# Computing the first four blocks of a scan's input projections one stage earlier, and passing them through DRAM

## The chip, the cores and the metric

The program runs on one core of a Trainium2 chip. The metric is device time in microseconds (us), the median of three runs. The engines are named PE (TensorE, matmuls), PEld (its weight loads), DVE (VectorE), ACT (ScalarE), POOL (GpSimd) and SP (SyncE, which issues most transfers). Each engine works through its own instructions in order; semaphores join them.

## The reference, cut to what matters

Input x has 4 x 1024 tokens of 256 channels. Eight layers follow each other; each adds to x. The change touches the fourth (a mixture of experts) and the fifth (a selective scan); the sixth runs interleaved with the fifth.

```
x = x + ln(mixture(ln(x)))
x = x + ln(scan_layer(ln(x)))
x = x + ln(ternary_mlp(ln(x)))

def mixture(x):            # 16 experts, the 2 best per token, and one shared
    w, i = top_k(sigmoid(x @ gate_w + gate_b), 2);  w = w / sum(w)
    return x + mlp_shared(x) + sum(w * mlp_i(x))        # mlp: (silu(x@wg) * (x@wu)) @ wd

def scan_layer(x):         # 256 -> 512 channels, 16 states
    xc, z = split(x @ in_proj_w.T)
    xs = silu(conv4(xc) + conv_b)
    dt, B, C = split(xs @ x_proj_w.T)
    dt = softplus(dt @ dt_proj_w.T + dt_proj_b)
    h[t] = exp(dt * A) * h[t-1] + dt * B * xs           # per channel and state
    y = (sum(h * C) + D * xs) * silu(z)
    return y @ out_proj_w.T
```

## The kernel before, in words

x stays in on-chip memory as `chip.x`, 32 tiles of 128 tokens; a block is four tiles (512 tokens), and there are NB = 8 blocks. All data of the parts shown is 32-bit floating point.

**The mixture** (`mixture`) routes the tokens, runs the experts over 80 blocks of gathered rows, and stores their outputs in DRAM as `y_rows`. Then comes its results stage, the one that the change rebuilds. For each block n:

- POOL issues eight indirect gathers (`results(n)`, L2108) that bring the rows of both choices into `got`, which is laid over the experts' up weights (in the trace it bears their name, `l1f_w`).
- PE computes the shared expert (`up`, L1833; `down`, L1841 and L1842). ACT takes the gate (`gate_rows`, L1905) and DVE multiplies (`hidden_rows`, L2034). `down` adds the normalised row (`acc`) by a matmul with the identity.
- DVE's `combine(n)` adds two scaled gathers (L2044) and takes the statistics of the post norm (L1586 to L1591). POOL raises to the power -1/2 (L1595), DVE makes the shift (L1601), ACT applies the norm (L1608) and DVE's `add` adds the result to `chip.x` (L2055).
- POOL's order is: results(0), results(1), then for each n the power of post norm n and results(n+2). At n = 7 it also does the scan's first norm (`following`).

**The scan and its MLP** (`scan_and_mlp`) begin when all engines have left the mixture. A head computes block 0's input: SP loads `w_in` and other weights, ACT normalises block 0 (`pre`, L1570), PE turns it (L3042), projects x (L3054) and z (L3061), ACT makes the 16 diagonals of the conv weights (L3314), DVE convolves (L3431), PE projects to `x_dbl` (L3098) and dt (L3105). `x_dbl`'s B and C rows go through DRAM and come back broadcast (`bc`).

The main loop has iterations n = 0 to 9, of UNITS = 64 units k each. Iteration n runs the scan of block n (states by channel tiles): ACT's exponentials (L3276), POOL's products `dbx` (L2968) and sums (L2978), DVE's scans (L3489) and multiplications by C (L3500). Fixed slots k (the tables `FUSED`, `ZERO`, `FIRST`) put the other work between the units: for block n+1 the pre norm, turning, x projection, convolution, `xs` and dt; for block n the z projection (`project_z`, L3081; ACT takes it with Silu at k = 12) and the gating of y (L3423); for block n-1 the output projection (L3114), post norm and residual, and then the MLP's turning (`turn_l`, L3042), pairs (L3137) and hidden layers (L3150); for block n-2 the rest of the MLP (L3126). Four shared PSUM banks pass PE's results to ACT and DVE. MLP weights stream from DRAM through a ring of four buffers. PE's queue for iteration n is: outputs(n-1), hidden 14 and 15 of n-2, z(n), dt(n), the MLP's output n-2, turn_l(n-1), pairs, and the hidden layers 0 to 12 of n-1 with turn, x projection, `x_dbl` and dt of n+1 among them.

Of the kernel before, what the change touches and what calls it, by code (L numbers as in the profile page):

```python
# [12 lines left out]
F32 = mybir.dt.float32  # L13
# [22 lines left out]
FAR_ROWS = 3 * SEQ_TILES  # L36

# [1596 lines left out]
def mixture(chip, name, gate_w, gate_b, w_up, wd, counts, ids, x_rows, y_rows, norms, following):  # L1634
# [12 lines left out]
    AHEAD = 4  # L1647
    with ExitStack() as ctx:
# [12 lines left out]
        later = [ScaledNorm(chip, s, f"pre{n}") for n in range(2, NB)]  # L1661
        turned_score = s.sb("turned_score", [P, 2, P])
# [27 lines left out]
        normed = wo[:, 1:1 + 2 * BT, :].rearrange("p (i k) d -> p i k d", i=2)  # L1690
        PS = chip.psum
# [19 lines left out]
        summed = s.sem("summed")  # L1711
        normed_ready, added = s.sem("normed_ready"), s.sem("added")
# [3 lines left out]
        def _(sp):  # L1716
# [14 lines left out]
            for b in range(BLOCKS):  # L1731
                sp.wait_ge(b_out, b + 1)
                sp.dma_start(y_rows[b * P:(b + 1) * P, :], out_b[:, b % AHEAD, :]).then_inc(b_put[b % AHEAD], 16)

        @block.tensor
        def _(pe):
# [100 lines left out]
            def down(n):  # L1837
                pe.wait_ge(h_ready, n + 1)
                wait(pe, out_used, n - 1)
                for k in range(BT):  # L1840
                    nc.tensor.matmul(outs[n % 2][:, k, :], chip.ident[:], acc[:, n * BT + k, :], start=True, stop=False)  # L1841
                    last = nc.tensor.matmul(outs[n % 2][:, k, :], h[:, n % 2, k * P:(k + 1) * P], wo[:, 0, :],  # L1842
                                            start=False, stop=True)
                last.then_inc(out_ready, 1)

# [3 lines left out]
            for n in range(NB):  # L1849
                down(n)  # L1850
                if n + 2 < NB:
                    up(n + 2)

        @block.scalar
        def _(act):
# [51 lines left out]
            gate_rows(0)  # L1907
            gate_rows(1)
            for n in range(NB):
                if n + 2 < NB:  # L1910
                    gate_rows(n + 2)
                wait(act, added, n - 1)
                posts[n % 2].scalar(act, n // 2, lambda k: acc[:, n * BT + k, :], lambda k: normed[:, n % 2, k, :])\
                    .then_inc(normed_ready, 1)

        @block.vector
        def _(v):
# [118 lines left out]

            def combine(n):
                v.wait_ge(got_ready[n % 4], 16 * CHOICES * BT * (n // 4 + 1))
                v.wait_ge(out_ready, n + 1)
                for c, (done, rows_of) in enumerate(((out_used, lambda k: outs[n % 2][:, k, :]),  # L2040
                                                     (summed, lambda k: acc[:, n * BT + k, :]))):
                    for k in range(BT):
                        t = n * BT + k
                        last = nc.vector.scalar_tensor_tensor(  # L2044
                            out=acc[:, t, :], in0=got[:, n % 4, c, k, :], scalar=share[:, t, c:c + 1], in1=rows_of(k),
                            op0=ALU.mult, op1=ALU.add)
                    last.then_inc(done, 1)
                    v.drain()
# [3 lines left out]
            def add(n):  # L2052
                v.wait_ge(normed_ready, n + 1)
                x = chip.x[:, n * BT:(n + 1) * BT, :]
                nc.vector.tensor_tensor(x, x, normed[:, n % 2], ALU.add).then_inc(added, 1)  # L2055

            hidden_rows(0)
            hidden_rows(1)
            for n in range(NB):
                if n == NB - 1:  # L2060
                    wait(v, added, 1)
                    following.statistics(v, lambda k: chip.x[:, k, :])
                combine(n)
                if n:
                    posts[(n - 1) % 2].vector(v, (n - 1) // 2)
                if n + 2 < NB:
                    hidden_rows(n + 2)
                if n >= 2:
                    add(n - 2)
            posts[(NB - 1) % 2].vector(v, (NB - 1) // 2)  # L2070
            add(NB - 2)
# [3 lines left out]
        def _(g):  # L2075
# [40 lines left out]
            for n in range(NB):  # L2116
                if n == NB - 1:
                    following.gpsimd(g, 0)
                posts[n % 2].gpsimd(g, n // 2)
                if n + 2 < NB:  # L2120
# [264 lines left out]
def windowed_core(chip, name, stacks, y, window, ahead):  # L2385
# [16 lines left out]
    with ExitStack() as ctx:  # L2402
# [226 lines left out]
    "z": 12,  # L2629
    "soften": [53, 13],  # L2630
# [43 lines left out]
        "turn": 9, "in": [13, 14, 27, 28], "conv": [19, 23, 32, 36], "xp_pe": 41, "dt_pe": 47}  # L2674
# [4 lines left out]
def scan_and_mlp(chip, name, a, m, pre, bias, following):  # L2679
# [22 lines left out]
    with ExitStack() as ctx:  # L2702
# [26 lines left out]
        first_loaded, xc_cleared = s.sem("first_loaded"), s.sem("xc_cleared")  # L2729
# [1041 lines left out]
```

## Time and profile before

| | |
|---|---|
| median of 3 runs | 4317.69 us (4316.76 to 4327.96) |
| the profiled execution's own time | 4321.57 us |
| its span | 4319.8 us |
| mean granted clock of TensorE | 0.963 |
| PE busy | 3980.5 us, 92% of the span |
| DVE busy | 3322.9 us, 77% |
| ACT busy | 2849.1 us, 66% |
| POOL busy | 2003.2 us, 46% |

Stages by time from the span's start: the mixture's experts end near 1423 us, its results stage runs to 1530.8 us, the scan's head from there to the first scan at 1570.9 us, the scan and MLP loop to about 3125 us. Busy shares are averages over stages with different limits, so each stage is to be read by itself. A row of a timeline gives start, duration, engine, line, operation, output and inputs, and in brackets how long the engine sat idle before it and what it waited for.

### The profile page before, as it was taken

How to read it: one execution, taken by the hardware profiler on the slowest of the kernel's cores; microseconds unless marked ns; L12 is line 12 of the kernel's file. 1: busy time of each engine (PE TensorE's matmuls, PEld its weight loads, DVE VectorE, ACT ScalarE, POOL GpSimd, SP SyncE). 2: the span in 40 equal slices, each digit the busy share in tenths (PEclk: the TensorE clock that was granted, in tenths of full speed). 3: DMA queues.
4: the chain of work that ended last, by engine and by line, in shares of the span. 5: the costliest groups of instructions: out<-in, count | busy, mean ns of one | idle time of the engine just before them, and what ended most of it. 6: DMA issues, size and time to landing. Idle time of an engine off the chain costs nothing. (4 is left out here: it accounts for less than half of the span.)

```text
span 4319.8 us, 100821 instructions
## 1 busy us (share of the span) xinstructions
PE 3980.5 (92%) x39417; PEld 2123.1 (49%) x39417; DVE 3322.9 (77%) x5680; ACT 2849.1 (66%) x4554; POOL 2003.2 (46%) x1898
## 2 busy tenths in 40 slices
PE   8899999988959757899999999999999999999897
PEld 4344444564538423354544445455454555555555
DVE  7899999686665569888888888886137888888586
ACT  5577777664553155888888888875125777777664
POOL 5222222251235635888888888886001222222332
PEclk9899999998979979899999999999998999999999
DMA  4211111105335345455565655654223222222100
GB/s 146 66 39 39 39 39 39 27 28 124 73 114 160 98 113 125 125 156 160 148 169 146 149 146 156 170 151 134 87 90 106 65 65 61 61 70 61 31 13 27
DMA packets 263805, 412.40 MB, mean 95 GB/s; under 512 B 52731, under 2 KB 139802, under 8 KB 263170
## 3 DMA queue, kind: packets, MB, share of 16 engines
q1 hardware_dynamic: 228966, 375.81, 32.1%
q0 software_dynamic: 6912, 18.88, 1.8%
q10 hardware_dynamic: 27456, 11.28, 1.2%
q8 instruction: 314, 5.14, 0.5%
q14 instruction: 157, 1.29, 0.1%
HBM read 351.85 MB, written 53.24 MB: 94 GB/s over the span
## 5 line engine op out<-in xcount | busy, mean ns | idle before, releaser
L2968 POOL TENSOR_TENSOR l_dbx<-l_u,l_bc 128x1024 f32<-128x1024 f32 x256 | 603.4, 2357 | 247.3 <-DVE banks L3489 84.3
L1169 DVE CUSTOM_DVE_ANT_0 banks<-banks,l3s_table 128x1024 f32<-128x1024 f32 x512 | 619.4, 1241 | 89.5 <-PE banks L1089 84.7
L1252 ACT ACTIVATE l3s_probs<-banks 128x512 f32<-128x512 f32 x1024 | 540.3, 595 | 204.1 <-PE banks L1118 100.8
L1164 DVE TENSOR_REDUCE l0s_peak<-banks 128x1 f32<-128x1024 f32 x512 | 605.3, 1214 | 58.3 <-PE banks L1089 57.9
L1252 ACT ACTIVATE l0s_probs<-banks 128x512 f32<-128x512 f32 x1024 | 535.7, 600 | 164.8 <-PE banks L1089 163.1
L3276 ACT ACTIVATE banks<-l_dt,l_decay 128x512 f32<-128x512 f32 x512 | 346.7, 687 | 221.6 <-DVE banks L3489 219.1
L2978 POOL TENSOR_TENSOR l_ys<-l_ys,l_hc 128x1024 f32<-128x1024 f32 x203 | 479.6, 2362 | 21.5 <-DVE l_hc L3500 21.4
L3150 PE MATMUL banks<-l_ha,l_ring 128*128 128x512 f32 x1024 | 446.6, 593 | 3.9 <-issue 3.9
L3150 PE MATMUL banks<-l_hb,l_ring 128*128 128x512 f32 x1024 | 443.1, 593 | 1.6 <-ACT l_hb L3241 0.8
L3489 DVE TENSOR_TENSOR_SCAN banks<-banks,l_carry,l_dbx 128x512 f32<-128x512 f32 x256 | 319.3, 1279 | 68.7 <-ACT banks L3276 61.8
L1089 PE MATMUL banks<-l3s_q_st,l3s_k_st 122*32 122x512 bf16 x4096 | 346.9, 381 | 4.8 <-ACT l3s_probs L1252 1.0
L3489 DVE TENSOR_TENSOR_SCAN banks<-banks,l_dbx 128x512 f32<-128x512 f32 x256 | 302.8, 1217 | 59.5 <-ACT banks L3276 53.7
L1089 PE MATMUL banks<-l0s_k_st,l0s_q_st 96*32 96x512 bf16 x4096 | 317.2, 387 | 15.8 <-PEq L711 13.4
L1089 PE MATMUL banks<-l3s_k_st,l3s_q_st 96*32 96x512 bf16 x4096 | 318.3, 387 | 7.1 <-PEq L711 3.6
L1089 PE MATMUL banks<-l0s_q_st,l0s_k_st 98*32 98x512 bf16 x4096 | 315.6, 382 | 5.8 <-ACT l0s_probs L1252 2.4
L3500 DVE TENSOR_TENSOR l_hc<-banks,l_bc 128x512 f32<-128x512 f32 x484 | 318.6, 676 | 0.4 <-issue 0.4
L3150 PEld LDWEIGHTS banks<-l_ha,l_ring 128*128 128x128 f32 x1024 | 193.9, 190 | 247.3 <-issue 247.2
L3150 PEld LDWEIGHTS banks<-l_hb,l_ring 128*128 128x128 f32 x1024 | 193.8, 190 | 245.9 <-issue 241.8
L1129 PE MATMUL banks<-l3s_probs,l3s_vs 128*32 128x256 f32 x4096 | 265.5, 378 | 0.8 <-ACT l3s_probs L1252 0.8
L1129 PE MATMUL banks<-l0s_probs,l0s_vs 128*32 128x256 f32 x4096 | 265.3, 379 | 0.8 <-ACT l0s_probs L1252 0.8
L3137 PE MATMUL banks<-l_xtl,l_ring 128*128 128x512 f32 x512 | 226.5, 601 | 18.7 <-DMA l_ring<-in_l2f_stream 8.6
L3276 ACT ACT_TABLE_LOAD x161 | 206.6, 1283 | 31.1 <-DVE banks L3489 28.2
(531 smaller groups left out, 7166.9 us busy)
## 6 DMA issues: line engine op xcount, KB each, us to landing
l_bc<-l_bc_rows SPq DMA_DIRECT2D x256, 512.0 KB, 5.4
l_ring<-in_l2f_stream SPq DMA_DIRECT2D x176, 512.0 KB, 6.4
l3s_table<-bias_table SPq DMA_DIRECT2D x16, 960.0 KB
qk_parts<-l0s_probs SPq DMA_DIRECT2D x96, 128.0 KB, 2.4
qk_parts<-l3s_probs SPq DMA_DIRECT2D x32, 384.0 KB, 3.5
y_rows<-l1f_out_b SPq DMA_DIRECT2D x80, 128.0 KB, 1.7
l0s_q_st<-qk_parts SPq DMA_DIRECT2D x64, 96.0 KB
l0s_k_st<-qk_parts SPq DMA_DIRECT2D x64, 96.0 KB
```

Of the source, the lines that this page charges most:

```text
L1089: last = nc.tensor.matmul(out[j:j + BLOCK, :], stationary[:, j:j + BLOCK], moving, start=start, stop=stop)
L1129: last = nc.tensor.matmul(outT[q * 32:(q + 1) * 32, :], vs[b % 2][:, kt, :], probs[b % 2][:, kt, q * QUARTER:(q + 1) * QUARTER], start=(kt ...
L1164: nc.vector.tensor_reduce(out=peak[:, b % 2, t:t + 1], in_=s1[t % 2], axis=AX, op=ALU.max, negate=True).then_inc(s1_used, 1)
L1169: nc.vector.tensor_tensor_reduce(out=s1[t % 2], in0=s1[t % 2], in1=rows, scale=1.0, scalar=LOW, op0=ALU.add, op1=ALU.max, accum_out=peak[: ...
L1252: nc.scalar.activation(columns(probs[b % 2][:, t, :], half * 512, (half + 1) * 512), scores, ACT.Exp, scale=scale).then_inc(s2_used, 1)
L2968: nc.gpsimd.tensor_tensor(dbx[:, at:at + 2], u[:, 2 * mh:2 * mh + 2], bc[:, load % BR, 0].unsqueeze(1).to_broadcast([P, 2, TB]), ALU.mult)\
L2978: nc.gpsimd.tensor_tensor(ys[:, 2 * mh:2 * mh + 2], ys[:, 2 * mh:2 * mh + 2], hc[:, at:at + 2], ALU.add)\
L3137: last = nc.tensor.matmul(banks[:, bank, :], w[:, at:at + P], xtl[:, c, :], start=(c == 0), stop=(c == KC - 1))
L3150: last = nc.tensor.matmul(banks[:, bank, :], w[:, c * P:(c + 1) * P], src[:, c, :], start=(c == 0), stop=(c == HT - 1))
L3276: nc.scalar.activation(banks[:, DA + m2, :], dt[:, mt], ACT.Exp, scale=decay[:, mt, st:st + 1])\
L3489: nc.vector.tensor_tensor_scan(out=banks[:, H + m2, :], data0=banks[:, DA + m2, :], data1=dbx[:, k % DR], initial=start, op0=ALU.mult, op1 ...
L3500: nc.vector.tensor_tensor(hc[:, k % CR] if st or n == 0 else ys[:, mt], banks[:, H + m2, :], bc[:, load % BR, 1], ALU.mult).then_inc(hc_re ...
```

## The change

The results stage of the mixture also computes, for blocks 0 to 3 (MADE = 4), the scan's pre norm, the turning and both halves of the input projection, and stores them in DRAM as `x_parts` and `z_parts` (1 MB for each block and half). The scan loads them instead of computing them.

In the results stage:

- `down` drops the identity matmul; DVE's new `add_shared(n)` adds the shared expert's output to `acc` (one instruction of 128x1024), and both gathers of `combine` then read and write `acc`.
- Two more norms (`pres`, SplitNorm). DVE's order is written out anew: `settle(n)` does the shifts of post n-1 and pre n-2, combine(n), add(n-1) and pre statistics of n-1. Each of the first eight shared steps comes first: settle(0) to settle(3) follow shared steps 1, 3, 5 and 7.
- POOL gets pres[n-1]'s power between post n's power and results(n+2), for n = 1 to 4; `following` goes.
- PE, after all shared work: for n = 0 to 3, eight transposes and eight projections of two accumulated matmuls each, through banks 4 to 7.
- ACT applies each pre norm (4 instructions), takes 2 turned tiles and 8 projections (x by Copy, z by Silu) a block, in an order written out by hand between the post norms.
- SP loads `w_in` into the freed expert weights, stores the eight parts, and waits for them to land before the stage can end.

In the scan: iterations 0 to 2 no longer do the pre norm, turn and project x for blocks 1 to 3, and iterations 1 to 3 no longer project and take z. SP loads z at k = 8 and x at k = 12. The head loads block 0's x and z. `take_x` for blocks under 4 is one ACT instruction from `xc` to PSUM. `w_in` is loaded last of the head's weights.

```diff
@@ mixture, sync
+            sp.dma_start(ahead_w, w_in.rearrange("(c p) n -> p c n", p=P)).then_inc(ahead_loaded, 16)
+            for n in range(MADE):
+                for kind, parts in enumerate((x_parts, z_parts)):
+                    sp.wait_ge(ahead_taken, n * UNITS + KC + (kind + 1) * CT)
+                    sp.dma_start(parts[n], stage[:, 2 * (n % 2) + kind]).then_inc(part_stored[2 * (n % 2) + kind], 16)
+            for done in part_stored:
+                sp.wait_ge(done, 16 * (MADE // 2))
@@ mixture, tensor
-                    nc.tensor.matmul(outs[n % 2][:, k, :], chip.ident[:], acc[:, n * BT + k, :], start=True, stop=False)
...
+            pe.wait_ge(h_ready, NB)
+            pe.wait_ge(ahead_loaded, 16)
+            for n in range(MADE):
+                turn_ahead(n)
+                project_ahead(n)
@@ mixture, scalar
+            def rows_ahead(n):
+                wait(act, ahead_filled, (n - 1) * UNITS + KC)
+                pres[n % 2].scalar(act, n // 2, lambda k: chip.x[:, n * BT + k, :], lambda k: ahead_rows[:, k, :])\
+                    .then_inc(ahead_ready, 1)
...
+            post_rows(1)
+            rows_ahead(0)
+            keep_ahead(0, 0, 4)
+            post_rows(2)
+            rows_ahead(1)
+            keep_ahead(0, 4, 10)
...
+            post_rows(6)
+            keep_ahead(2, 8, 10)
+            keep_ahead(3, 0, 4)
+            post_rows(7)
+            keep_ahead(3, 4, 10)
@@ mixture, vector
+            def settle(n):
+                if n:
+                    shifts(n - 1)
+                combine(n)
+                if n:
+                    add(n - 1)
...
             for n in range(NB):
-                if n == NB - 1:
-                    wait(v, added, 1)
-                    following.statistics(v, lambda k: chip.x[:, k, :])
-                combine(n)
...
+                add_shared(n)
                 if n + 2 < NB:
                     hidden_rows(n + 2)
+                if n % 2:
+                    settle(n // 2)
+            for n in range(NB // 2, NB):
+                settle(n)
+            shifts(NB - 1)
             add(NB - 1)
@@ mixture, gpsimd
                 posts[n % 2].gpsimd(g, n // 2)
+                if 0 < n <= MADE:
+                    pres[(n - 1) % 2].gpsimd(g, (n - 1) // 2)
@@ scan_and_mlp, sync
+            def load_x(n):
+                wait(sp, xc_kept, n)
+                sp.dma_start(xc[:, :, TAPS - 1:], x_parts[n]).then_inc(xc_loaded, 16)
+            def load_z(n):
+                wait(sp, y_ready, 2 * n)
+                sp.dma_start(zs[:], z_parts[n]).then_inc(z_loaded, 16)
...
+                    if 0 < n < MADE and k == AT["z_load"]:
+                        load_z(n)
+                    if n and n + 1 < MADE and k == AT["x_load"]:
+                        load_x(n + 1)
@@ scan_and_mlp, tensor
-                if n < NB:
+                if MADE <= n < NB:
                     for i in range(CT):
                         project_z(n, i)
...
-                    if q in AT["in"] and more:
+                    if q in AT["in"] and more and n + 1 >= MADE:
                         project_x(n + 1, AT["in"].index(q))
@@ scan_and_mlp, scalar
             def take_x(n, i):
+                if n < MADE:
+                    bank = bank_for(act, f"in{n}.{i}")
+                    act.wait_ge(xc_loaded, 16 * (n + 1))
+                    nc.scalar.activation(banks[:, bank, :], xc[:, i, TAPS - 1:], ACT.Identity,
+                                         scale=taps[:, i, TAPS - 1:TAPS], bias=conv_b[:, i:i + 1]).then_inc(tap_done, 1)
...
-                    if k == AT["z"] and 0 < n < NB:
+                    if k == AT["z"] and MADE <= n < NB:
```

## Rows read from the trace of the kernel before

**Rows 1.** Busy time by stretch: window, length, busy time of each engine, granted clock, DMA share, GB/s.

```profile
1440.00:1520.00 80.00, 45.57 (x137) 29.38 (x135) 50.67 (x162) 14.84 (x29) 62.15 (x61) 0.85 0.31 89
...
1537.40:1543.40 6.00, 5.97 (x10) 2.67 (x11) 0.20 (x1) 5.99 (x19) 0.00 (x0) 0.70 1.06 320
...
1877.00:2056.00 179.00, 175.97 (x468) 86.58 (x467) 152.29 (x223) 149.24 (x188) 148.74 (x78) 1.00 0.58 155
```

**Rows 2.** Timeline of the scan loop, PE.

```profile
2077.33 7.07 PE L3114 MATMUL banks<-l_w_out,l_xs 128*128 128x256 f32 x32
...
2097.97 7.03 PE L3081 MATMUL banks<-l_xt,l_w_in 128*128 128x512 f32 x16
...
2121.62 1.04 PE L3042 MATMUL banks<-ident,l_rows 128*128 128x128 f32 x8
...
2209.00 3.60 PE L3098 MATMUL banks<-l_xs,l_w_x 128*96 128x512 f32 x8
```

**Rows 3.** Timeline of the scan loop, ACT.

```profile
2103.78 1.28 ACT L3241 ACT_TABLE_LOAD   x1
2105.08 2.06 ACT L3241 ACTIVATE l_zs<-banks 128x512 f32<-128x512 f32 x4
2107.16 1.28 ACT L3276 ACT_TABLE_LOAD   x1
...
2118.41 2.06 ACT L1570 ACTIVATE l_rows<-x,l_pre_l_shift,l_pre_l_rstd 128x256 f32<-128x256 f32 x4
...
2207.49 0.60 ACT L3262 ACTIVATE l_xs<-banks 128x512 f32<-128x512 f32 x1
```

**Rows 4.** Timeline of the scan loop, DVE.

```profile
2074.94 1.23 DVE L3423 TENSOR_TENSOR l_xs<-l_xs,l_zs 128x1024 f32<-128x1024 f32 x1
...
2109.18 1.29 DVE L3489 TENSOR_TENSOR_SCAN banks<-banks,l_carry,l_dbx 128x512 f32<-128x512 f32 x1 [2.87 <-ACT banks L3276]
...
2110.97 1.39 DVE L126 BATCH_NORM_STATS2 l2n_pre_stats<-x 128x6 f32<-128x256 f32 x4
```

**Rows 5.** Timeline of the scan loop, POOL.

```profile
2113.73 1.18 POOL L1560 TENSOR_TENSOR l2n_pre_rstd<-l2n_pre_mean_var,eps 128x4 f32<-128x4 f32 x1
...
2117.59 2.35 POOL L2968 TENSOR_TENSOR l_dbx<-l_u,l_bc 128x1024 f32<-128x1024 f32 x1
```

**Rows 6.** Timeline of the results stage, POOL.

```profile
1425.94 0.95 POOL L2108 DMA_INDIRECT l1f_w<-y_rows,l1f_put  x1 [14.02 <-DMA y_rows<-l1f_out_b]
...
1445.88 1.06 POOL L1595 TENSOR_TENSOR l1f_post_rstd<-l1f_post_shift,mhalf 128x4 f32<-128x4 f32 x1
...
1515.28 0.95 POOL L2108 DMA_INDIRECT l1f_w<-y_rows,l1f_put  x1 [0.30 <-issue]
```

**Rows 7.** Timeline of the results stage, PE and DVE.

```profile
1430.51 0.69 DVE L2034 TENSOR_TENSOR l1f_h<-banks,l1f_gate 128x512 f32<-128x512 f32 x1 [2.74 <-ACT l1f_gate L1905]
...
1433.14 3.60 PE L1833 MATMUL banks<-l1f_xt,l1f_w 128*128 128x512 f32 x8
...
1441.28 1.41 DVE L1586 BATCH_NORM_STATS2 l1f_post_stats<-l1f_acc 128x6 f32<-128x256 f32 x4 [0.44 <-issue]
...
1518.12 1.66 DVE L2044 SCALAR_TENSOR_TENSOR l1f_acc<-l1f_w,l1f_share,banks 128x256 f32<-128x256 f32 x4 [3.46 <-DMA l1f_w<-y_rows,l1f_put]
...
1529.59 1.23 DVE L2055 TENSOR_TENSOR x<-x,l1f_wo 128x1024 f32<-128x1024 f32 x1 [1.07 <-ACT l1f_wo L1608]
```

**Rows 8.** DMA issues by name: size of one and time from issue to landing.

```profile
l_w_in<-in_l2s_w_in SPq DMA_DIRECT2D x1, 1024.0 KB, 5.0
```

**Rows 9.** Timeline of the scan's head, ACT, PE and DVE.

```profile
1537.41 4.78 ACT L3314 ACTIVATE l_ha<-ident,l_taps 128x128 f32<-128x128 f32 x16 [1.56 <-DMA l_conv_b<-in_l2s_conv_b]
...
1543.43 9.37 DVE L3431 SCALAR_TENSOR_TENSOR banks<-l_xc,l_taps,banks 128x512 f32<-128x512 f32 x12 [1.49 <-ACT banks L3255]
...
1570.89 2.35 DVE L3489 TENSOR_TENSOR_SCAN banks<-banks,l_dbx 128x512 f32<-128x512 f32 x2 [2.52 <-POOL l_dbx L2968]
...
1537.43 8.90 PE L3054 MATMUL banks<-l_xt,l_w_in 128*128 128x512 f32 x16 [2.22 <-DMA l_conv_b<-in_l2s_conv_b]
```

More of the change, by code:

```diff
@@ L1661, in mixture @@
         later = [ScaledNorm(chip, s, f"pre{n}") for n in range(2, NB)]
+        pres = [SplitNorm(chip, s, f"scan{i}") for i in range(2)]
         turned_score = s.sb("turned_score", [P, 2, P])
@@ L2044, in combine @@
                         last = nc.vector.scalar_tensor_tensor(
-                            out=acc[:, t, :], in0=got[:, n % 4, c, k, :], scalar=share[:, t, c:c + 1], in1=rows_of(k),
+                            out=acc[:, t, :], in0=got[:, n % 4, c, k, :], scalar=share[:, t, c:c + 1], in1=acc[:, t, :],
                             op0=ALU.mult, op1=ALU.add)
-                    last.then_inc(done, 1)
-                    v.drain()
+                last.then_inc(summed, 1)
+                v.drain()
                 wait(v, normed_ready, n - 1)
@@ L2629 @@
     "z": 12,
+    "z_load": 8,
+    "x_load": 12,
     "soften": [53, 13],
@@ L2783, in scan_and_mlp @@
             for q in range(MAIN):
-                groups += [f"turn{n + 1}.{c}" for c in range(KC) if q == AT["turn"] and more]
+                groups += [f"turn{n + 1}.{c}" for c in range(KC) if q == AT["turn"] and more and n + 1 >= MADE]
                 groups += [f"in{n + 1}.{AT['in'].index(q)}"] if q in AT["in"] and more else []
@@ L2855, in tokens, with taps_before @@
             return chip.x[:, n * BT:(n + 1) * BT, :]
+        def taps_before(n):
+            return (n - 1 if n > 1 else n) * CT
         rel_emb, onehot, sides_in, table, bands, far = bias
@@ L3306, in logarithm @@
                 nc.scalar.activation(dt[:, 2 * half:2 * half + 2], eb[:], ACT.Ln).then_inc(ln_ready, 1)
-            pre.scalar(act, 0, lambda k: tokens(0)[:, k, :], lambda k: rows[:, k, :]).then_inc(rows_ready, 1)
-            for c in range(KC):
-                take_turned(0, c)
-            act.wait_ge(first_loaded, 16 * 3)
-            for j in range(TAPS):
-                for c in range(CT):
-                    last = nc.scalar.activation(diagonals[:, j, c, :], chip.ident[:], ACT.Copy, scale=taps[:, c, j:j + 1])
-            last.then_inc(diagonals_ready, 1)
+            act.wait_ge(first_loaded, 16 * 2)
             for i in range(CT):
@@ L3319, in _ @@
                 silu_x(0, i)
-            for i in range(CT):
-                act.wait_ge(z_filled, i + 1)
-                nc.scalar.activation(zs[:, i, :], banks[:, DA + i, :], ACT.Silu).then_inc(z_kept, 1)
+                for j in range(TAPS):
+                    last = nc.scalar.activation(diagonals[:, j, i, :], chip.ident[:], ACT.Copy, scale=taps[:, i, j:j + 1])
+            last.then_inc(diagonals_ready, 1)
             take("xp0", x_dbl[:])
```

202 lines of the change are left out of this document (125 added, 77 removed).

## The prediction

> **What bounds the kernel now.** I read the busy time by stretch first [rows 1]. In the scan loop PE is busy 175.97 of 179 us and DVE, ACT and POOL 149 to 152 each: PE looks like the bound, and the change takes work from it. In the results stage nothing is busy all the time; POOL is nearest, 62 of 80. So work goes from a full stage into one with room, and the questions are how much of PE's time comes back and whether the room is where the work lands.
>
> For the first question I read the loop engine by engine. PE starts the outputs of block 2 at 2077.33 [rows 2]; DVE finishes the y that they need at 2074.94 + 1.23 = 2076.2 [rows 4]. PE starts x_dbl at 2209.0 [rows 2]; ACT finishes its last input at 2207.49 + 0.60 = 2208.1 [rows 3]. So at the two points of an iteration where PE takes what the scan gives, PE comes only 1.2 and 0.9 us after it. The scan's own chain through ACT, DVE and POOL is as long as PE's queue. **A faster PE waits at these two points; what comes back is what the chain gets shorter.**
>
> For the results stage the chain of gathers is what to see: first at 1425.94, last at 1515.28 [rows 6]. 63 gathers and six powers lie between; at 1.25 us a gather (0.95 and 0.30 idle) and some 1.3 a power with its gap [rows 6] that is 79 + 8 = 87 of 89.3 us. The gathers issue back to back, and all else in the stage hides behind them.
>
> **The change, part by part.** Times are positions in the profiled execution.
>
> *Results stage, POOL.* Four more powers, 1.15 each: 4.6 us, all in front of a gather. And each new power waits for DVE, with the next eight gathers queued behind it. DVE per block: combine twice 1.66 and a gap, 3.4; statistics 2.1 with aggregates (first part 1.41); add 1.23; shift 0.6 [rows 7]. New: add_shared (128x1024, priced like the add, 1.25), the multiply of the shared expert 0.69, pre statistics 2.1, pre shift 0.6. Together 12.0 a block, against POOL's 10.0 + 1.1 + 1.2 + 0.3 = 12.6; but in the first periods DVE does two shared steps, 14 us. Walking the order written in the diff: PE does an `up` in 3.6 [rows 7] and the halved `down` in 1.7 (half of the 3.3 that 16 rows of 256 take now, estimated from the halving of the instructions), so the second pair of shared steps ends at 1441.7, and settle(0) begins there although its gathers landed at 1437.4. Its statistics come at 1447.4, POOL is free at 1446.1: stall 1.4. Pre statistics of block 0 come at 1461.7, of block 1 at 1475.7, of block 2 at 1488.4; POOL is ready for them at 1460.0, 1474.4 and 1488.4: stalls 1.7, 1.4 and 0. Sum 4.6 + 4.5 = 9.1, of which 0.5 overlaps with gaps: the last gathers are 8.6 late. The bounds: 4.6 (no stall), and 20 if each store of 1 MB holds a block's gathers (a rival below). At the end the last power no longer waits behind `following`: POOL has it at 1523.7 and does it at 1525.7 now, 2 us back. Block 7's x is done 6.5 us later than now, near 1537.3.
>
> *Results stage, PE and ACT.* A block ahead is 8 transposes in 1.04 and 16 rows of 512 in 7.03 at the full clock, as the same work takes in the loop [rows 2], and ACT's 2.1 + 10 x 0.52. In periods of 13 us both fit. Where PE has been idle it starts at half its clock: the x projection after the stage took 8.90 instead of 7.03 [rows 9]. I count that for block 3 alone, 1.3 us, in the 1537.3 above. Six copies follow (3.1): ACT ends at 1540.
>
> *The end of the stage.* SP must see the last 1 MB land. The trace has no store of that size; a load of 1 MB lands in 5.0 us [rows 8]. I take 5.2, since the x part of block 3 is still under way. Stage end 1545.2, against 1530.8 now: **+14.3**, between +10 (no stall, full clock) and +23 (half clock throughout). All engines wait at this border, so nothing hides it.
>
> The Trainium skill, "DMA: Bandwidth & Descriptors", Anatomy of one DMA, gives about 2.0 us fixed and 436 GB/s, most of it the receipt when DRAM is the target. By that a store is an estimated 4.4 us, and the stage would end 0.8 earlier. It speaks against the change as the row does: a stage's border after a store is paid in full.
>
> *Head.* Now the convolution starts at 1543.43, 12.6 after the stage, because x is projected (1537.4) and ACT makes 16 diagonals (4.78) first [rows 9]. After: two small loads, then x of block 0, 1 MB, in by 6.4; one ACT instruction of 0.73: DVE starts at 7.3, 5.3 earlier. The diagonals go between the convolutions. PE is then cold: x_dbl's last part and two dt each at half the clock give back some 0.4. The rest of the chain to the first scan (27.5 us, to 1570.89) is unchanged. **-4.9**, between -3 (2 MB more in SP's queue delay the first B and C rows) and -7.
>
> *Iteration 0.* DVE loses 1.8 us of pre statistics, but the next exponential is ready only when they end: **0**, at most -1.9.
>
> *Iteration 3: z goes.* PE loses 7.03 [rows 2]. ACT loses 1.28 + 2.06 + 1.28 = 4.6 us [rows 3], in front of an exponential for which DVE waits 2.87 [rows 4]. ACT's turn comes 4.6 earlier, pre_l (2118.41 [rows 3]) ends near 2116, and PE, whose output matmuls end by 2115 without z, turns there instead of at 2121.62 [rows 2]: 5.3. Then POOL: the product for scan pair 8 starts at 2117.59 [rows 5], ends at 2119.95 and is now needed at 2118.3; POOL ran without a gap up to it, through the pre power (block 4's, which stays). So DVE gains 3.1 there and little more behind. **-3.5**, from 2 to 6.
>
> *Iteration 2: z, x, turn and pre norm go.* PE loses 7.03 + 7 + 1.04 = 15. The same 5.3 to the turning; POOL's limit is gone, because the pre power (1.18 and what follows, 3.9 us up to 2117.59 [rows 5]) goes too; DVE loses 1.39 and more of statistics [rows 4], ACT 2.1 of the norm, 1.1 of xt, and 2 of xc copies, about a third of these where DVE waits. **-6.5**, from 3 to 11.
>
> *Iteration 1.* As iteration 2, but POOL gives the pair at k = 12 late (DVE waits 2.9 for it) and that stays. **-5.5**, from 2 to 10.
>
> The loads in the loop, three z and two x of 1 MB, fall where POOL is some 10 us behind the B and C loads: **0**, up to +2 each if that cover were gone.
>
> The Trainium skill, "ScalarE: Activation LUTs", What ACT_TABLE_LOAD costs, counts 1.28 and a drain of 1.38 for a switch. The row does not agree: the Silu starts at once when its load ends [rows 3]. By the rule each z would cost 2.8 more, an estimated 8 us over three iterations, and the scan would gain that much more at most.
>
> *Sum.* +14.3 - 4.9 - 0 - 5.5 - 6.5 - 3.5 = **-6.1**. The profiled execution took 4321.57 (span 4319.8 and 1.8 around it); it would take 4315.5. It stands 3.9 above the median of the runs, 4317.69, so for the median I predict **4312**.
>
> **Rivals.**
>
> *PE alone paces the loop.* For it: 175.97 of 179 busy [rows 1]. Then its whole relief returns: z 3 x 7.0, x 2 x 7.0, turns 2 x 1.0, less what is idle anyway in iteration 1: 36 instead of 15.5. Against: the slacks of 1.2 and 0.9 us. Time 4312 - 20.5 = 4291.
>
> *The loop gives next to nothing.* POOL, which had no gap from 2095 to 2133, and DVE take up what ACT gives; 5 us return, not 15.5. Against: DVE's waits for ACT. Time 4322.
>
> *Slower: the stores hold the gathers.* Six of the eight stores are under way before the last gather has landed. They use the same 16 DMA engines, and a gather that lands late makes combine, statistics and the power late, behind which POOL's next gathers stand. 1 MB at the 320 GB/s of the head's busiest stretch [rows 1] is 3.3 us; six are 20. Time 4312 + 20 = 4332. It decides from 6.1 us, two stores fully exposed. Against: the DMA share is 0.31 there [rows 1], and DVE comes to most blocks after their gathers have landed.
>
> **How the numbers follow.** A measurement of this kernel tells about 0.3%, 13 us. The likeliest case 0.58, its own range 4301 to 4321 from the bounds of stage and loop together; PE alone 0.12; next to nothing 0.15; the stores 0.13; the 0.02 left is for what I don't see. Faster by over 13 us: PE alone (0.12) and the low fifth of the likeliest (0.11), 0.23. Slower by over 13: over half of the stores' case (0.08) and the high ends of the others (0.06), 0.14. Within: the rest, 0.63. The range 4294 to 4329 leaves out most of PE alone and half of the stores' case.
>
> **What the profile after would show.** The last gather at 1524 (1515.28 now); POOL's waits for pre statistics of 1 to 2 us; add of block 7 near 1536; stage end 1545; DVE's first convolution 7.3 after it and the first scan 35 after. In the loop, the distance between starts of L3114 for blocks 0 to 1, 1 to 2 and 2 to 3 (184.4, 185.0, 185.3 now) at 179, 178.5 and 182, PE waiting for DVE's y and for ACT's xs, and 185 again from block 3 on. I am wrong if these distances fall by 10 or more (PE alone), if they don't move, or if the gathers end after 1530.

## The result, and the profile after

The change makes the kernel a little slower or leaves it as it was. In the first measurement it took 4329.6 us (14 runs, 4325.4 to 4335.2) against 4320.1 for the kernel before (14 runs): ratio 1.0018, 95% interval 1.0011 to 1.0026. Measured again with the experiments, it took 4327.7 against 4331.1: ratio 0.9991, interval 0.9981 to 1.0001. The changed kernel kept its time; the kernel before was 11 us slower on each of the three chips of the experiments. So single times are compared below only within a chip, and reasons are read from the lengths of the stages. The forecast was 4312, range 4294 to 4329; the first measurement is just above it. The ratios leave out one execution of the new order below, which took 4446.9 us at a granted clock of 0.908 against 0.96.

The table has these lengths in us, from the trace of each kernel: from the first gather of the results stage to SP's first load of the scan, from there to DVE's first scan, and then from POOL's last product of one iteration to that of the next.

```
                         results  head  it 0   it 1   it 2   it 3
before                    105.1   39.8  122.2  182.3  185.2  185.1
before, second trace      106.9   40.8  122.2  183.6  185.3  184.9
after                     124.2   33.6  122.2  182.7  178.9  184.8
after, second trace       124.4   33.7  122.2  182.6  179.2  187.1
block 3 left out          113.5   32.7  122.5  183.2  179.2  184.9
new ACT order             116.6   35.0  122.2  180.6  179.1  184.6
three blocks ahead        114.0   32.9  122.5  182.3  183.4  185.0
two blocks ahead          112.3   32.7  122.2  181.8  184.8  184.9
order + extra, it 0       115.3   32.8  122.2  182.0  179.0  185.0
order + later remainder   113.7   33.6  122.2  182.4  179.0  185.0
order + extra, it 0, 3    121.7   34.8  122.2  180.3  179.1  182.1
order + extra, it 0 to 3  114.4   33.2  122.2  179.9  179.6  182.6
```

Each row is one traced execution. Such an execution stands up to 8.5 us off the median of its kernel (4326.2 against 4317.7 for "order + extra, it 0, 3"; 4326.2 against 4331.7 for the second trace of before), and the stretches outside the table, which no edit touches, differ by up to 14 us between the traces. The rows tell where time went; which kernel has the better median they don't tell.

The span grew from 4319.8 to 4328.1. By the table: results stage +19.0, head -6.2, iteration 0 0.0, iteration 1 +0.4, iteration 2 -6.2, iteration 3 -0.3; the remaining +1.6 lie before and behind. Predicted were +14.3, -4.9, 0, -5.5, -6.5 and -3.5.

**Results stage.** POOL's part went as forecast. The timeline of POOL after answers to [rows 6]:

```profile
1426.28 0.94 POOL L2208 DMA_INDIRECT l1f_w<-y_rows,l1f_put  x1 [14.10 <-DMA y_rows<-l1f_out_b]
...
1447.62 1.04 POOL L1596 TENSOR_TENSOR l1f_post_rstd<-l1f_post_shift,mhalf 128x4 f32<-128x4 f32 x1 [1.40 <-DVE l1f_post_shift L1592]
...
1461.74 1.00 POOL L1596 TENSOR_TENSOR l1f_scan_rstd<-l1f_scan_shift,mhalf 128x4 f32<-128x4 f32 x1 [1.36 <-DVE l1f_scan_shift L1592]
...
1522.67 1.24 POOL L2208 DMA_INDIRECT l1f_w<-y_rows,l1f_put  x1 [0.30 <-issue]
```

POOL waits 1.40 and 1.36 us (forecast 1.4 and 1.7), then 0.39 where 1.4 was forecast, and the last gather is at 1522.7 (forecast 1524). DVE's last add (row below) ends at 1539.0 (forecast 1537.3). What is late is PE. Timelines of PE, DVE, ACT and SP of the changed kernel:

```profile
1469.81 1.06 PE L1871 MATMUL banks<-ident,l1f_rows 128*128 128x128 f32 x8 [0.97 <-ACT l1f_rows L1609]
1471.62 10.57 PE L1880 MATMUL banks<-l1f_out_b,l1f_wo 128*128 128x512 f32 x24 [0.74 <-ACT l1f_out_b L1972]
1482.51 3.70 PE L1880 MATMUL banks<-l1f_out_b,l1f_wo 128*128 128x512 f32 x8 [0.33 <-ACT l1f_xt L1972]
1486.05 1.04 PE L1871 MATMUL banks<-ident,l1f_rows 128*128 128x128 f32 x8
1494.06 16.06 PE L1880 MATMUL banks<-l1f_out_b,l1f_wo 128*128 128x512 f32 x32 [6.97 <-ACT l1f_out_b L1972]
1509.95 1.04 PE L1871 MATMUL banks<-ident,l1f_rows 128*128 128x128 f32 x8
1514.12 15.70 PE L1880 MATMUL banks<-l1f_out_b,l1f_wo 128*128 128x512 f32 x32 [3.12 <-ACT l1f_out_b L1972]
1529.65 1.04 PE L1871 MATMUL banks<-ident,l1f_rows 128*128 128x128 f32 x8
1531.48 14.00 PE L1880 MATMUL banks<-l1f_out_b,l1f_wo 128*128 128x512 f32 x32 [0.79 <-ACT l1f_out_b L1972]
...
1537.80 1.22 DVE L2143 TENSOR_TENSOR x<-x,l1f_wo 128x1024 f32<-128x1024 f32 x1 [2.87 <-ACT l1f_wo L1609]
...
1545.52 0.60 ACT L1972 ACTIVATE l1f_xt<-banks 128x512 f32<-128x512 f32 x1 [1.12 <-PE banks L1880]
...
1546.14 0.32 SPq L1748 DMA_DIRECT2D z_parts<-l1f_xt  x1
1550.46 0.33 SPq L2988 DMA_DIRECT2D l_taps<-in_l2s_taps  x1
```

A block's projection is 32 rows and 14.0 us at the full clock, not 16 rows and 7.03. (A matmul of 128x512 in the program stands in the trace as two rows: z alone is eight of them, 16 rows in [rows 2]; x and z are sixteen.) With the two gaps of 6.97 and 3.12 PE comes to block 3 at 1531.5. The store is issued at 1546.1 and the stage ends 4.3 us later, at 1550.5. Four stores of each kind landed in a median of 4.3 and 4.2 us (forecast 5.2). The estimate that the prediction worked out by the Trainium skill, "DMA: Bandwidth & Descriptors", Anatomy of one DMA, was 4.4. The section gives its fit for transfers that GpSimd issues; these are issued by SP, and their 4.2 and 4.3 us agree with it.

**Head.** Answers to [rows 9]; ACT, then DVE:

```profile
1556.85 2.89 ACT L3357 ACTIVATE banks<-l_xc,l_conv_b,l_taps 128x512 f32<-128x512 f32 x4 [10.74 <-DMA l_xc<-x_parts]
...
1557.77 9.37 DVE L3537 SCALAR_TENSOR_TENSOR banks<-l_xc,l_taps,banks 128x512 f32<-128x512 f32 x12 [18.74 <-ACT banks L3357]
...
1584.08 2.35 DVE L3595 TENSOR_TENSOR_SCAN banks<-banks,l_dbx 128x512 f32<-128x512 f32 x2 [2.52 <-POOL l_dbx L3089]
```

The convolution starts 7.3 us after the stage's end, as forecast, and the first scan 33.6 after it.

**Loop.** PE's output projections, which [rows 2] shows for block 2 at 2077.33, come 179.0 us apart from block 1 to 2 (forecast 178.5), but 182.2 from 0 to 1 and 185.5 from 2 to 3 (forecast 179 and 182). Windows of iteration 3 in the changed kernel (columns as in [rows 1]), and below them PE's timeline:

```profile
2115.00:2120.00 5.00, 5.00 (x25) 4.39 (x24) 4.85 (x11) 4.95 (x5) 4.85 (x5) 1.00 0.11 23
2120.00:2125.00 5.00, 2.74 (x16) 1.97 (x14) 5.00 (x4) 2.96 (x7) 4.71 (x6) 1.00 0.02 9
2125.00:2130.00 5.00, 2.60 (x3) 1.17 (x4) 5.00 (x9) 4.39 (x9) 5.00 (x3) 0.63 0.63 211
2130.00:2135.00 5.00, 5.00 (x9) 2.09 (x8) 4.61 (x12) 3.20 (x4) 5.00 (x3) 0.69 0.62 205
2135.00:2140.00 5.00, 5.00 (x13) 2.28 (x12) 2.54 (x3) 1.20 (x2) 4.86 (x4) 1.00 0.34 107
```

```profile
2123.00 1.09 PE L3163 MATMUL banks<-ident,l_rows 128*128 128x128 f32 x8 [1.35 <-ACT l_rows L1571]
2127.39 13.80 PE L3252 MATMUL banks<-l_xtl,l_ring 128*128 128x512 f32 x25 [3.31 <-DVE l_hb L3551]
```

In the coordinates of before (less 6.8) PE turns at 2116.2 instead of 2121.62, which is the 5.4 us of the forecast. But PE now waits, and the pairs behind the wait run with a granted clock of 0.63 to 0.69, partly at the lower of its two levels (1.2 GHz). DVE then waits 2.68 us for a pair; before it waited 0.34 at this place. The row of DVE in the kernel before, and in the changed kernel:

```profile
2130.22 0.75 DVE L3510 SCALAR_TENSOR_TENSOR l_ha<-banks,l_sc,l_hb 128x512 f32<-128x512 f32 x1 [0.34 <-PE banks L3137]
...
2137.46 0.75 DVE L3616 SCALAR_TENSOR_TENSOR l_ha<-banks,l_sc,l_hb 128x512 f32<-128x512 f32 x1 [2.68 <-PE banks L3252]
```

In five windows of 5 us of the kernel before, from 2107 to 2132, PE was busy 24.66 of 25 us and had 1.00. DVE and POOL at the same place:

```profile
2117.00 2.78 DVE L3572 SCALAR_TENSOR_TENSOR l_ys<-l3p_rows,l_ys 128x1024 f32<-128x1024 f32 x1
2119.86 3.22 DVE L3576 TENSOR_TENSOR l_ys<-l_u,l_ys 128x1024 f32<-128x1024 f32 x1
...
2116.35 2.35 POOL L3089 TENSOR_TENSOR l_dbx<-l_u,l_bc 128x1024 f32<-128x1024 f32 x1
2118.66 3.34 POOL L3099 TENSOR_TENSOR l_ys<-l_ys,l_hc 128x1024 f32<-128x1024 f32 x1
```

Before, these two DVE operations took 1.30 and 1.23 us, beside POOL's small pre-norm operations. Two suspects, then, for the gain that did not come: this collision, and PE's clock.

### The profile page after: what moved, and what is told of

It is laid out like the page before. It is cut to its first block and busy times, and to the rows that moved or that the text cites. A ratio compares the mean times of both kernels' runs of the same rounds, so it can differ in the third digit from the quotient of the medians.

```text
span 4328.1 us, 100716 instructions
## 1 busy us (share of the span) xinstructions
PE 3973.4 (92%) x39353; PEld 2110.8 (49%) x39353; DVE 3341.3 (77%) x5708; ACT 2843.9 (66%) x4548; POOL 1999.6 (46%) x1886
```

## The experiments

The first four share a chip. The next three share one with the second measurement of the changed kernel, and the last two (extra matmuls in iterations 0 and 3, and 0 to 3) with the second trace of the kernel before. The kernel before had 4330.6, 4331.1 and 4330.5 us on them.

**What ends the results stage.** One run leaves block 3's work out of the stage, one changes the order in which ACT serves it:

```diff
@@ block 3 left out
-                    sp.wait_ge(ahead_taken, n * UNITS + KC + (kind + 1) * CT)
+                    sp.wait_ge(ahead_taken, min(n * UNITS + KC + (kind + 1) * CT, 3 * UNITS))
...
-            for n in range(MADE):
+            for n in range(MADE - 1):
                 turn_ahead(n)
...
-            rows_ahead(3)
-            keep_ahead(3, 0, 4)
-            keep_ahead(3, 4, 10)
@@ new ACT order
             keep_ahead(0, 4, 10)
+            keep_ahead(1, 0, 2)
             post_rows(3)
             rows_ahead(2)
-            keep_ahead(1, 0, 5)
+            keep_ahead(1, 2, 9)
             post_rows(4)
-            keep_ahead(1, 5, 10)
+            keep_ahead(1, 9, 10)
+            keep_ahead(2, 0, 2)
             rows_ahead(3)
-            keep_ahead(2, 0, 3)
+            keep_ahead(2, 2, 8)
             post_rows(5)
-            keep_ahead(2, 3, 8)
-            post_rows(6)
             keep_ahead(2, 8, 10)
             keep_ahead(3, 0, 4)
+            post_rows(6)
+            keep_ahead(3, 4, 10)
             post_rows(7)
-            keep_ahead(3, 4, 10)
```

> Left out: block 3's turning, projections and copies in the results stage; its two parts are stored from block 1's instead, with the same eight stores, and everything behind is as in the changed kernel. Theory A (PE's 14 us of block 3 set the end): stage end at the last add of DVE plus a landing, near 1540, and 4320. Theory B (stores and gathers set it): no change, 4329.

> The order of ACT alone is changed, so that block 1's and block 2's turned rows are kept before the next norms and PE does not wait 6.97 and 3.12 us for them. Theory A (PE's work of block 3, begun late, sets the stage's end): PE's last projection ends near 1535 instead of 1545.5, the last add of DVE (1539.0) becomes what ends the stage, stage end near 1540.5 instead of 1550.4, head and loop as they were, so 9.5 us less than the changed kernel: 4320. Theory B (the eight stores and the gathers' chain hold the end, PE only fills the time): stage end moves under 3 us, time above 4326.

Left out: stage 113.5 instead of 124.2, 4317.6 us, ratio to before 0.9970 (0.9959 to 0.9982). SP, and DVE's last add, of that kernel:

```profile
1526.62 0.92 SPq L1748 DMA_DIRECT2D z_parts<-l1f_xt  x1
1536.66 0.34 SPq L2985 DMA_DIRECT2D l_taps<-in_l2s_taps  x1
...
1533.69 1.23 DVE L2140 TENSOR_TENSOR x<-x,l1f_wo 128x1024 f32<-128x1024 f32 x1 [2.20 <-ACT l1f_wo L1609]
```

All eight stores are issued by 1527.5, 9 us ahead of the end; the stage ends 1.7 us after the last add. So neither the number of stores nor the gathers hold the end, but block 3's late work does. The last gather is issued 96.8 us after the first, against 96.4 in the changed kernel, and a gather lands in a median of 2.8 us in the changed kernel as in the one before: the stores don't hold the gathers.

New order: 4321.7 us, ratio 0.9978 (0.9967 to 0.9989). PE and SP:

```profile
1492.62 14.00 PE L1880 MATMUL banks<-l1f_out_b,l1f_wo 128*128 128x512 f32 x32 [0.79 <-ACT l1f_out_b L1972]
...
1510.47 15.70 PE L1880 MATMUL banks<-l1f_out_b,l1f_wo 128*128 128x512 f32 x32 [2.97 <-ACT l1f_out_b L1972]
...
1528.43 14.00 PE L1880 MATMUL banks<-l1f_out_b,l1f_wo 128*128 128x512 f32 x32 [1.39 <-issue]
...
1543.09 0.32 SPq L1748 DMA_DIRECT2D z_parts<-l1f_xt  x1
1547.42 0.34 SPq L2989 DMA_DIRECT2D l_taps<-in_l2s_taps  x1
```

From the first gather (1430.81 here) PE comes to block 3 at +97.6 instead of +105.2, 7.6 us earlier, and the stage ends 7.6 earlier. Theory A holds in the main: PE's late block 3 sets the end. My 1535 for PE's end was 3 us too early in the same coordinates, since one gap of 2.97 stayed, and the last store still lands after DVE's last add. Four more traces with this order, below, have a stage of 113.7, 114.4, 115.3 and 121.7, so its 116.6 is one of a spread.

**Fewer blocks ahead.** MADE is 3, and 2; ACT's list without the blocks that go.

> Three blocks ahead instead of four. Theory A: one block less takes the 14 us at the end away, stage end near 1539 (minus 11); iteration 2 of the loop then drops z alone, which gave nothing in iteration 3, so its 6.0 us are lost: 4329.6 - 11 + 6 = about 4325. If dropping z alone is worth 3.5 us, as was predicted for iteration 3, 4321.5. If PE alone paced the loop, iteration 2 would lose 8 of PE's work and the time would be near 4327.

> Two blocks ahead. Theory A: stage end is DVE's last add, 2 us earlier than with four since two powers and statistics are gone: 1537.5 (minus 13); head as in the changed kernel (minus 6.4 against before); iterations 1 to 3 give nothing, so the 6.2 us of the loop are lost but for z of block 1: 4329.6 - 13 + 6 = about 4323. If each iteration gave what was predicted (z alone 3.5), 4319.

4320.5 us (ratio 0.9972, 0.9962 to 0.9981) and 4320.2 (0.9980, 0.9970 to 0.9989). The rows of the table are what tells. Results stage 114.0 and 112.3, near the 113 and 111 that the expectations imply. Dropping z alone gives 1.7 us in iteration 2 of the first and 0.5 in iteration 1 of the second (2.3 without a loss of 1.8 at its start, below), against 0.3 in iteration 3 of the changed kernel: nowhere the 3.5 that I had put down, and not the same twice (the clock tells why, below). Against before, the two medians are 10.1 and 10.4 us lower, where the lengths in the table, against its second trace, say 3.6 and 5.0. That is within what one traced execution can stand off its median; more I can't say.

**The loop: collision or clock.** First the collision measured by itself, in a stage of its own in the kernel before:

```diff
+        def dve_sbuf(i):
+            return nc.vector.tensor_tensor((d0, d1)[i % 2][:], a[:], b[:], ALU.add)
...
+        def pool_long(i):
+            return nc.gpsimd.tensor_tensor((r0, r1)[i % 2][:], p[:], q[:], ALU.mult)
...
+        phases = [(dve_sbuf, None), (None, pool_long), (dve_sbuf, pool_long), (dve_scalar, None), (dve_scalar, pool_long),
+                  (dve_psum, None), (dve_psum, pool_long), (dve_scan, None), (dve_scan, pool_long),
+                  (dve_stats, None), (dve_stats, pool_long), (None, pool_small), (dve_sbuf, pool_small)]
```

> The kernel before with a short measuring stage ahead of the mixture, whose results are not used: eight DVE instructions of one kind alone, then beside eight POOL products of 128x1024, for five kinds. If DVE's operations with both inputs and the output in SBUF have to take turns with POOL's, a 128x1024 sum takes 1.2 alone and about 2.4 to 3.3 beside POOL, and POOL's product grows from 2.35 to over 3; those with an operand in PSUM (product, scan) stay at 0.68 and 1.2. If it is only a matter of the data that the two share in the loop, all keep their times here.

DVE and POOL, eight instructions in a group, alone and then together:

```profile
1281.92 9.67 DVE L1650 SCALAR_TENSOR_TENSOR price_t<-price_t 128x1024 f32<-128x1024 f32 x8 [2.36 <-POOL price_tiny L1697]
1291.84 24.18 DVE L1650 SCALAR_TENSOR_TENSOR price_t<-price_t 128x1024 f32<-128x1024 f32 x8
...
1343.55 9.60 DVE L1657 TENSOR_TENSOR_SCAN banks<-banks,price_t 128x512 f32<-128x512 f32 x8 [13.83 <-POOL price_tiny L1697]
1353.40 9.60 DVE L1657 TENSOR_TENSOR_SCAN banks<-banks,price_t 128x512 f32<-128x512 f32 x8
...
1235.94 18.96 POOL L1664 TENSOR_TENSOR price_t<-price_t 128x1024 f32<-128x1024 f32 x8 [9.78 <-DVE price_stats L1680]
1291.91 26.30 POOL L1664 TENSOR_TENSOR price_t<-price_t 128x1024 f32<-128x1024 f32 x8 [9.80 <-DVE price_stats L1680]
```

DVE's operation with all operands in SBUF goes from 1.21 to 3.02 us beside POOL's product, and the product from 2.37 to 3.29. The scan and the product with PSUM keep their times, and so do the statistics (3.23 us for eight, alone and beside). The collision is real, with the loop's own sizes.

Is it what took iteration 3's gain? One run moves the second remainder of iteration 3 by two units, on top of the new order:

```diff
         def slot(n, name):
 
+            if n == 3 and name == "remainder":
+                return 14
```

> On top of the new ACT order: in iteration 3 alone DVE does its second remainder at unit 14 instead of 12, beside POOL's small powers and not beside its long product and sum. If the collision of DVE's two 128x1024 operations with POOL's long ones (2.78 and 3.22 us instead of 1.30 and 1.23) ate iteration 3's gain, the two take 1.3 and 1.2 and the iteration takes 181.5 to 182.5 instead of 184.7. If POOL's own chain of products gives the pace there, it stays at 184.5 or more.

Iteration 3 stayed at 185.0 (4322.1 us, ratio 0.9980, 0.9969 to 0.9990). The first of the two operations took 1.22, the second still 3.21, for POOL's small operations were just over, and POOL's next product and sum took 3.32 and 3.33. The collision had only moved, so this run is inconclusive on the collision. It shows one thing more: PE's wait before the pairs, which ends with DVE's `l_hb`, was 3.95 us here instead of 3.31, and its clock over ten us behind it 0.66, as without the edit.

The clock instead: PE gets matmuls whose results are overwritten, where it would wait.

```diff
@@ end of iteration 0
+                if 54 <= k < UNITS - 2:
+                    bank = bank_for(pe, "fill")
+                    for _ in range(2 if k < 58 else 1):
+                        last = nc.tensor.matmul(banks[:, bank, :], chip.ident[:], xs[1][:, 0, :], start=True, stop=True)
...
@@ iteration 3, before the turning
+                    if n == 3:
+                        bank = bank_for(pe, f"turn_l{b}.0")
+                        for _ in range(3):
+                            nc.tensor.matmul(banks[:, bank, :], w_in[:, 0, 0:P], w_in[:, 0, 0:TB], start=True, stop=True)
                     pe.wait_ge(rows_l_ready, n)
```

A first form had the iteration 0 part alone, with an extra matmul between the last sums too:

> On top of the new ACT order: PE does two to one extra identity matmuls into a free bank after each of the last ten sums of iteration 0 (their result is not used). If the end of iteration 0 is late because PE's last four sums run at half the clock (3.78 instead of 1.98 us), they take 1.98 in this run and DVE's wait before the gating of block 0 is 1.5 instead of 3.27 us; the time is that of the new order or 1.8 us less. If the wait has another cause, it stays 3.27 or grows by the extra matmuls.

> On top of the new ACT order: extra matmuls between the sums at the end of iteration 0 (none before the last pair of sums) and three extra matmuls of 128x512 (2.6 us) in iteration 3 before the turning for the MLP, where PE otherwise waits 1.35 us before and 3.31 us behind it. Their results are overwritten. Theory C (with z gone PE waits, its granted clock falls to 0.63 to 0.69 between 2125 and 2135 and the pairs run at half the clock, which costs the 3 us that the ACT relief had given): PE keeps the full clock there, iteration 3 takes 181.5 to 182.5 instead of 184.7, block 0's gating waits 1.5 instead of 3.27; the time is 4 to 5 us under the new order alone. Theory D (the collision of DVE and POOL alone ate it): iteration 3 stays at 184.7.

In the first form (4319.5 us, ratio 0.9977, 0.9964 to 0.9990) DVE's wait before the gating of block 0 fell from 3.27 to 2.33, of which an extra matmul ahead of the last sum is 0.86. In the second it is 1.47, the value of the kernel before. The second took 4317.7 us, ratio 0.9968 (0.9958 to 0.9978), and its iteration 3 182.1 instead of 184.6. Its windows, and below them the timelines of PE and DVE:

```profile
2127.00:2132.00 5.00, 2.68 (x13) 1.49 (x12) 5.00 (x9) 3.33 (x7) 4.85 (x5) 1.00 0.50 104
2132.00:2137.00 5.00, 5.00 (x13) 2.28 (x12) 4.84 (x11) 3.87 (x6) 5.00 (x3) 1.00 0.89 315
```

```profile
2125.16 2.74 PE L3331 MATMUL banks<-l_w_in 128*128 128x512 f32 x6
2127.73 1.04 PE L3164 MATMUL banks<-ident,l_rows 128*128 128x128 f32 x8
2131.09 19.12 PE L3253 MATMUL banks<-l_xtl,l_ring 128*128 128x512 f32 x44 [2.32 <-DVE l_hb L3564]
...
2120.69 2.80 DVE L3585 SCALAR_TENSOR_TENSOR l_ys<-l3p_rows,l_ys 128x1024 f32<-128x1024 f32 x1
2123.56 3.22 DVE L3589 TENSOR_TENSOR l_ys<-l_u,l_ys 128x1024 f32<-128x1024 f32 x1
...
2137.65 1.41 DVE L3629 SCALAR_TENSOR_TENSOR l_ha<-banks,l_sc,l_hb 128x512 f32<-128x512 f32 x2
```

DVE's two operations still take 2.80 and 3.22, and the gain is there all the same, though PE has 2.6 us more to do. The clock is 1.00 where it was 0.63 to 0.69, and DVE's wait of 2.68 us for a pair is gone. Theory C holds, and the collision, my own first reading, falls as what took the gain by itself. Whether it has a part in PE's wait is not tested: the two long operations, 3.5 us longer than before, stand ahead of the `l_hb` for which PE waits. (This run's results stage of 121.7 is no effect of the edit: ACT stood 3.49 us before block 3's turned rows for a cause the trace does not name, and block 3's projections took 16.42.)

The same in iterations 1 and 2, two extra matmuls before each of the hidden layers 1 to 4:

> As the run before, and two extra matmuls of 128x512 before each of the MLP's hidden layers 1 to 4 in iterations 1 and 2, in place of the x projections that were there before the change. Theory C: iteration 1, whose clock fell to 0.66 in its second half, keeps 1.00 from there on; but since DVE and POOL pace it, not PE, it gains at most 1 us (182.4 to 181.5), and iteration 2 stays at 179. If PE's work itself were what counts, both would be longer by 3 us or more.

4315.2 us, ratio 0.9964 (0.9953 to 0.9976): the lowest median here. Its interval overlaps those of the new order alone (0.9978) and of the run above, so what the extra matmuls give is read from the iterations' lengths and not from the medians. Iteration 1 took 179.9, iteration 2 179.6. The 14 us of extra matmuls cost nothing that shows in the one and 0.5 in the other.

The traces hold a check of theory C that needs no edit. In every iteration 2 or 3 from which z alone is gone, PE waits before the pairs; how much of the ten us behind this wait it spends at the lower clock differs, and the length of the iteration goes with it. Windows of the changed kernel, of "three blocks ahead" (iteration 2) and of "order + extra, it 0, 3", and below them all nine traces:

```profile
2125.00:2135.00 10.00, 7.61 (x11) 3.26 (x12) 9.61 (x20) 7.59 (x12) 10.00 (x5) 0.66 0.63 208
...
1935.00:1945.00 10.00, 7.91 (x15) 3.59 (x16) 9.17 (x22) 7.97 (x13) 10.00 (x5) 0.83 0.62 205
...
2128.00:2138.00 10.00, 7.68 (x24) 3.68 (x22) 9.84 (x21) 8.19 (x13) 9.85 (x8) 1.00 0.70 211
```

```
granted clock            iteration's length
1.00                     182.1, 182.6 (the two with extra matmuls in iteration 3)
0.83                     183.4 (three blocks ahead, iteration 2)
0.66                     184.6, 184.8, 184.9, 185.0, 185.0 (changed kernel and four variants)
0.66, and 0.83 in ten
us that start 28 later   187.1 (changed kernel, second trace)
```

**The changed kernel and the kernel before, once more.**

> The changed kernel unaltered, beside the next two, to have its ratio under the same conditions. The first measurement gave a ratio of 1.0018 to the kernel before; from the traces (stage +19.0, head -6.2, loop -6) 1.0018 again. If the traces leave out something that differs between chips, the ratio moves and the comparisons of the experiments have to be made against this run.

> The kernel before unaltered, for a trace on this chip. Its median was 4320 in the first measurement and 4331 in the two of the experiments, while the changed kernel kept 4329.6 and 4327.7. If a stage of it that the change removes is sensitive to the chip, its results stage, head or iterations 0 to 3 are 5 to 10 us longer here than in the first trace; if not, the difference lies outside them and the traces' stage lengths hold.

The changed kernel's iteration 3 took 187.1 there. Its clock was 0.89 and 0.77 in the windows of 10 us from 2120 and 2130, which is the stretch seen in the first trace, and 0.83 in the one from 2150, which the first trace doesn't have. The rest repeats. The kernel before was 1.8 us longer in the results stage, 1.0 in the head and 1.3 at the end of iteration 0. That is 4.1 of the 4.6 us between its two traced executions (4321.6 and 4326.2). But its median on these chips is 4331, and what makes up the rest of the 11 us no trace shows.

## Why the prediction was wrong

Of the 17.6 us between the forecast and the first measurement, 2.4 are the base: three executions of the kernel before had a median of 4317.7, fourteen 4320.05. The change was forecast at -5.7 and measured at +9.6. The traces show 14.4 of these 15.2 us: iteration 1 5.9, the results stage 4.7, iteration 3 3.2, iteration 2 0.3, the head -1.3, and 1.6 outside. Iterations 1 and 3 fell outside the ranges that the prediction gave them; the results stage, at +19.0, stayed inside its +10 to +23. That the second measurement's ratio, 0.9991, is near the forecast's 0.9987 is luck: the kernel before was slower there, and the lengths of the stages missed the forecast as in the first measurement.

**What bounds the kernel.** "A faster PE waits at these two points" was right, and it waits elsewhere too. What I did not see is that the waiting is not free: it lowers PE's clock for the work behind it.

**Results stage, PE and ACT: a step that failed.** "A block ahead is 8 transposes in 1.04 and 16 rows of 512 in 7.03" counts one half of the projection. The trace had it: [rows 2] show 16 rows for z alone; x and z are 32 rows and 14.0 us (sixteen matmuls of the program, two rows each). "In periods of 13 us both fit" falls with it: 15 us of PE a block, and ACT's norms, which stand in front of the turned rows, add gaps of 6.97 and 3.12. Block 3 ended the stage 124.2 us after the first gather instead of 119.3 (1545.2 less 1425.94); leaving it out gave back 10.7. Against the forecast of +14.3 the stage came out at +19.0. The mechanism (the last block's store and border in full) was right, its size was not.

**Results stage, POOL and DVE.** Right: the stalls (3.5 us in all, 4.5 forecast), the last gather and the last add, each within 1.7 us.

**End of the stage, head.** The store landed in 4.3, not 5.2, and the head gave 6.2 instead of 4.9. Both are small errors to the good side.

**Iteration 0: 0.** Within it, right. At its end PE's last four sums took 3.78 instead of 1.98 us, and block 0's gating waited 3.27 instead of 1.47. That happened in the changed kernel and in four variants, one of them with the new order and the same iteration 0 as the new order alone, where it did not happen; the second trace of the kernel before lost 1.3 there. So it depends on where the clock happens to fall; with the extra matmuls it is gone in both traces that have none ahead of the last sums.

**Iteration 2: -6.5.** -6.2, right. POOL's products show where: 2.9 us at pair 8, where the pre power went, and 2.4 at pair 12.

**Iteration 3: -3.5, a step that failed.** -0.3. The turning came 5.4 us earlier (forecast 5.3), and DVE's scan of pair 8 began 1.9 us earlier (forecast 3.1), with the extra matmuls and without. "So DVE gains 3.1 there and little more behind" priced all of PE's work behind the turning at the full clock. It was not: the pairs ran partly at the lower one, DVE waited 2.68 us for them, and at pair 9 the gain is 0.1 us; with the clock kept up it is 2.9 there, and iteration 3 gives 2.5 to 3.0.

**Iteration 1: -5.5, the step with the largest miss.** +0.4. Of the 5.9 us, 1.8 are the clock at its start. POOL's products then gained 1.9 us at pair 8, the removed pre power again, lost 1.1 at pair 12 and gained 0.6 later; the loss at pair 12 is 0.5 and 0.0 in "order + extra, it 0, 3" and "it 0 to 3". The rest is the term "As iteration 2": even in the fastest kernel it gives 2.4 of 5.5. In the kernel before, iteration 1 is not the full stage that [rows 1] shows, whose window lies in iteration 2:

```profile
1693.00:1875.00 182.00, 152.80 (x356) 69.81 (x357) 154.27 (x191) 135.95 (x173) 144.87 (x72) 0.91 0.50 132
```

PE already had 29 us free there and a granted clock of 0.91. That its relief was worth less for this reason is argued, not shown; some 3 us of the miss stay open.

**Rivals.** PE alone as the pace fell: 36 us less work gave 6, and in the fastest kernel, where iterations 1 to 3 give 10.5 of the forecast 15.5, 14 us of extra matmuls over iterations 1 and 2 were hidden but for 0.5. The stores did not hold the gathers. "The loop gives next to nothing" came nearest, by another mechanism than the one that I gave it.

## What to carry to other kernels

Before moving work into a stage with room, count its rows against a row of the trace for the same work, and ask which engine will do the last item; an average of busy time doesn't show that the last block starts late. When work is taken from a matmul engine that is nearly full, price the rest of its queue at the lower clock wherever it will now wait; if that queue is on the path, a few matmuls in the wait can pay for themselves (2.6 us of them shortened iteration 3 by 2.5). And read the row of each iteration that changes: the one next to the measured window may be another kind of stage.

## What the runs showed of the hardware

- PE's granted clock falls behind short waits. After 1.35 and 3.31 us of waiting it was 0.63 and 0.69 in the next two windows of 5 us; with 2.6 us of matmuls in the first wait, and 2.32 us of waiting left, it was 1.00.
- DVE and POOL slow each other when both of DVE's inputs lie in SBUF: 1.21 us became 3.02 beside POOL's 2.37, which became 3.29. By the Trainium skill, "SBUF — State Buffer", SBUF: two separate sides, the two share a pair of ports that one of them holds for a whole instruction. Strict turns would give an estimated 3.58 (1.21 + 2.37); the trace comes near it from below. It agrees in what is exempt: operations with one SBUF input kept their 0.67 and 1.20 us.
- A load of 1 MB behind others lands late: x and z parts 8.7 and 8.4 us (median of four), `w_in` at the end of the head's queue 9.5, against 5.0 as the first of the head's loads [rows 8].
- The kernel before took 4320 us in the first measurement and 4331 on each of three chips later, the changed kernel 4329.6 and 4327.7. Traces show 4 of the 11 us.
